# Picking each expert's tokens with the value columns stationary and the one-hot columns moving

## The chip, the cores and the metric

The kernel runs on one core of a Trainium2 chip. The metric is the device time of one execution in microseconds (us); lower is better. Engines are TensorE (PE, with its weight loads shown apart as PEld), VectorE (DVE), ScalarE (ACT), GpSimd (POOL) and SyncE (SP, which only issues DMAs here).

## The reference, cut to what matters

A graph layer over 1250 nodes and 21250 edges comes first; then a layer of 16 experts, in which every expert takes the 156 tokens with the largest affinity. The change touches only the choice of tokens in the second part:

```python
logits = jnp.einsum('bsd,de->bse', x, gate_weight)
affinity = jax.nn.softmax(logits, axis=-1).transpose(0, 2, 1)
gating, index = jax.lax.top_k(affinity, k)          # k = 156 of 1250 tokens
x_in = jnp.take_along_axis(x[:, None, :, :], index[..., None], axis=2)
h = jax.nn.gelu(jnp.einsum('bekd,edh->bekh', x_in, w1) + b1[None, :, None, :])
x_e = jnp.einsum('bekh,ehd->bekd', h, w2) + b2[None, :, None, :]
weighted = gating[..., None] * x_e
out = out.at[jnp.arange(Bx)[:, None], idx_flat].add(vals_flat)
```

## The kernel before, in words

The program has four stretches: layer norm and a table of rows in DRAM; 34 steps over the edges; two dense layers with batch norm; and, from about 397 us, the gate and the experts. Every engine has its own instruction list, written out by hand, and they meet through semaphores (`wait_ge`, `then_inc`). There is no scheduler: the order of the calls in `expert(e)` of each engine is the order of its work.

At the end of the gate, `slot` holds for each of the 1250 tokens (125 partitions by NT = 10 tiles) and each expert the place that the token takes among the expert's K = 156, or a number that matches no place. Then, for each expert e:

- `choose(e)` on VectorE (L1148 to L1155) makes the one-hot matrix `pick`: ten `tensor_scalar` compare `iota_slot` with the slot of a tile's tokens, 125 tokens by 156 places in fp16 each.
- `pick_tokens(e)` on TensorE (L1459 to L1467) multiplies it with `tok_aff`, which holds three values for a token and expert: the token's number and its affinity in two fp16 parts. The stationary operand is a half of `pick` (125 by KH = 78) and the moving one `tok_aff` (125 by 3). There are two halves and ten tiles, so 20 matmuls; the result `picked` lies in bank 1 as 78 partitions by 6.
- `indices(e)` on VectorE (L1157 to L1165) makes from it the gate values `gat` (through `gat_high`) and the row numbers `idx`: three short instructions.
- `gather(e)` on GpSimd (L466) fetches the 156 token rows by two indirect DMAs into `xg`, a ring of four; `turn_rows(e)` (L1469) turns them with eight transposes into banks 1 and 0, and `columns(e)` copies one bank by VectorE (L1167) and one by ScalarE (L704).
- `up(e, half)` (L1478) is 16 fp32 matmul instructions for each half, `gelu` on ScalarE and `low_h` on VectorE (L1181) make the hidden values in two fp16 parts, and `down(e)` (L1489, its matmuls are in `product`, L1300) is 48 fp16 matmuls of 156 moving columns. Its second half waits for `h_low` of the second half, which `low_h(e, 1)` gives.
- `turn_back(e)` (L1504) turns the result with eight transposes, `weigh` on VectorE and ScalarE multiplies by the gate, and `scatter` on GpSimd adds the rows into the output.

TensorE's order in `expert(e)` is `up(e, 0)`, `pick_tokens(e + 3)`, `turn_back(e - 1)`, `up(e, 1)`, `turn_rows(e + 1)`, `down(e)`. VectorE's is `indices(e + 3)`, `weigh(e - 1)`, `low_h(e, 0)`, `choose(e + 4)`, `columns(e + 1)`, `low_h(e, 1)`, `down_low(e + 1)`. So picks run three experts ahead. The picks of experts 0 to 2 stand in front of the loop, with `indices(0)` to `indices(2)` interleaved with `choose(2)` and `choose(3)` on VectorE; `down_low(0)` and `columns(0)` follow them there. `turn_rows(e)` waits for `idx_ready` of the picks issued before it, since it writes bank 1, in which `picked` lies; for expert 0 that is the third one.

The last lines of `turn_rows` and of `pick_tokens` before the matmuls say this:

```python
pe.wait_ge(xg_in[e % XR], e // XR * 32 + 32)
pe.wait_ge(idx_ready, min(e + 3, EX))
pe.wait_ge(pick_ready, e + 1)
```

Of the kernel before, what the change touches and what calls it, by code (L numbers as in the profile page):

```python
# [8 lines left out]
F32 = mybir.dt.float32  # L9
# [9 lines left out]
def gnn_ffn_kernel(nc, x, src, dst, edge_attr, W_e, b_e, W1, b1, g1, beta1, W2, b2, g2, beta2, eps,  # L19
# [5 lines left out]
    NT = N // P  # L25
# [9 lines left out]
    EX = gate_w.shape[1]  # L35
    K = N // EX * 2
    KH = K // 2
# [37 lines left out]
    with ExitStack() as ctx:  # L75
        def sb(name, shape, dt):
            return ctx.enter_context(nc.sbuf_tensor(name, shape, dt))

        def sem(name):
            return ctx.enter_context(nc.semaphore(name))  # L80

        bank = [ctx.enter_context(nc.psum_tensor(f"bank{i}", [128, 512], F32)) for i in range(8)]
# [66 lines left out]
        ident = sb("ident", [128, 128], F32)  # L149
# [36 lines left out]
        tok_aff = sb("tok_aff", [P, NT, EX, 3], F16)  # L186
# [19 lines left out]
        slot = sb("slot", [P, EX, NT], F32)  # L206
        idx = sb("idx", [KH, EX, 2], U32)
        gat = sb("gat", [KH, EX, 2], F32)
        gat_high = [sb(f"gat_high{b}", [KH, 2], F32) for b in range(2)]

        silu = [aggT[:, i, 0:CH[2][1]] for i in range(HK)]
# [21 lines left out]
        pick, xg, xT, hT, h32, yT, yw = [], [], [], [], [], [], []  # L233
# [53 lines left out]
        assert 3 * N + NT * 128 <= NT * H  # L287
        aff_lanes = rows_z2[0:P, 2 * N:2 * N + NT * 128].rearrange("p (t e l) -> p t e l", t=NT, e=EX)

        picked = bank[1][0:KH, 320:326]  # L290
        b1c, g1c, be1c = (colA[:, i * F1:(i + 1) * F1] for i in range(3))
        b2c, g2c, be2c = (colA[:, 3 * F1 + i * HK:3 * F1 + (i + 1) * HK] for i in range(3))

# [25 lines left out]
        kept = sem("kept"); kth_ps = sem("kth_ps"); count_ps = sem("count_ps")  # L319
        above_ready = sem("above_ready"); above_ps = sem("above_ps"); taken_ready = sem("taken_ready")  # L320
        taken_ps = sem("taken_ps");
        pick_ready = sem("pick_ready"); pick_ps = sem("pick_ps"); idx_ready = sem("idx_ready")
        xg_in = [sem(f"xg_in{b}") for b in range(XR)]
        ew_in = [[sem(f"ew_in{b}{m}") for m in range(2)] for b in range(RH)]
        W1_hi = sem("W1_hi"); W1_lo = sem("W1_lo"); W2_hi = sem("W2_hi"); W2_lo = sem("W2_lo")
# [432 lines left out]
        def _(dve):  # L758
# [389 lines left out]
            def choose(e):  # L1148
# [5 lines left out]
                                             None, ALU.is_equal)  # L1154
                last.then_inc(pick_ready, 1)  # L1155

            def indices(e):  # L1157

                dve.wait_ge(pick_ps, e + 1)
                v = picked.rearrange("p (a c) -> p a c", a=2)  # L1160
                dve.tensor_scalar(gat_high[e % 2][:], v[:, :, 1], 1.0 / A_SCALE, None, ALU.mult).then_inc(gat_step, 1)
                dve.wait_ge(gat_step, e + 1)
                dve.scalar_tensor_tensor(out=gat[:, e, :], in0=v[:, :, 2], scalar=1.0 / A_SCALE, in1=gat_high[e % 2][:],
                                         op0=ALU.mult, op1=ALU.add).then_inc(gat_ready, 1)
                dve.tensor_copy(idx[:, e, :], v[:, :, 0]).then_inc(idx_ready, 1)  # L1165
# [15 lines left out]
            def low_h(e, half):  # L1181
                b, f = e % 2, slice(half * 2, half * 2 + 2)
                dve.wait_ge(h_high, e * 2 + half + 1)
                dve.tensor_tensor(hT[b][:, 1, f, :], h32[b][:, f, :], hT[b][:, 0, f, :],
                                  ALU.subtract).then_inc(h_low, 1)
# [8 lines left out]

            def expert(e):
                if e + 3 < EX:
                    indices(e + 3)
                if e >= 1:
                    weigh(e - 1)
                low_h(e, 0)  # L1200
                if e + 4 < EX:
                    choose(e + 4)
                if e + 1 < EX:
                    columns(e + 1)
                low_h(e, 1)
                if e + 1 < EX:
                    down_low(e + 1)
# [2 lines left out]
            choose(0)  # L1210
            choose(1)
            for e in range(3):
                indices(e)
                if e < 2:
                    choose(e + 2)
# [8 lines left out]
        def _(pe):  # L1224
            pe.wait_ge(consts, 5)

            for n, (i, bk) in enumerate(((1, bank[5]), (0, bank[2]))):
                pe.wait_ge(ends_f_ready, n + 1)
                for j in range(J):
                    last = pe.transpose(bk[0:P, j * SB:(j + 1) * SB],  # L1230
                                        ends_f[i].rearrange("s (p j) -> s j p", j=J)[:, j, :], ident[0:SB, 0:SB])
# [12 lines left out]
            for t in range(2):  # L1244
# [4 lines left out]
                      start=True, stop=True).then_inc(zero_ps, 1)  # L1249
# [94 lines left out]
            for k in range(HK):  # L1344
                pe.wait_ge(h_hi, k + 1)
                for f in range(F1):
                    pe.matmul(bank[f][:, 0:nn], W1_16[:, 0, k, f * 128:(f + 1) * 128], h16[:, 0, k, :],  # L1347
                              start=(k == 0), stop=False, skip_group_check=True)
            pe.wait_ge(h_lo, 1)
            for f in range(F1):  # L1350
                for i, j in ((1, 0), (0, 1)):
                    for k in range(HK):
                        last = pe.matmul(bank[f][:, 0:nn], W1_16[:, i, k, f * 128:(f + 1) * 128], h16[:, j, k, :],  # L1353
                                         start=False, stop=(j == 1 and k == HK - 1), skip_group_check=True)
# [104 lines left out]
            def pick_tokens(e):  # L1459
                pe.wait_ge(pick_ready, e + 1)  # L1460
                if e >= 1:
                    pe.wait_ge(idx_ready, e)
                for a in range(2):
                    for t in range(NT):
                        last = pe.matmul(picked[:, 3 * a:3 * a + 3], pick[e % 2][:, t, a * KH:(a + 1) * KH],  # L1465
                                         tok_aff[:, t, e, :], start=(t == 0), stop=(t == NT - 1))
                last.then_inc(pick_ps, 1)  # L1467

            def turn_rows(e):  # L1469
                pe.wait_ge(xg_in[e % XR], e // XR * 32 + 32)  # L1470
                pe.wait_ge(idx_ready, min(e + 3, EX))
                for a in (1, 0):
                    for k in range(HK):
                        last = pe.transpose(bank[a][:, k * KH:(k + 1) * KH],  # L1474
                                            xg[e % XR][:, a, k * 128:(k + 1) * 128], ident[0:KH, 0:KH])
                    last.then_inc(xT_ps, 1)

            def up(e, half):  # L1478
                if half == 0:
                    pe.wait_ge(xT_sb, e * 2 + 2)  # L1480
                    pe.wait_ge(ew_in[e % RH][0], e // RH * 16 + 16)
                for f in range(half * 2, half * 2 + 2):
                    for k in range(HK):
                        last = pe.matmul(bank[2 + half][:, f % 2 * K:(f % 2 + 1) * K],  # L1484
                                         e32[e % RH][:, 0, k, f * 128:(f + 1) * 128], xT[e % 2][:, k, :],
                                         start=(k == 0), stop=(k == HK - 1), skip_group_check=True)
                    last.then_inc(h_ps, 1)
# [16 lines left out]
            def turn_back(e):  # L1504
                pe.wait_ge(yT_sb, e * HK + HK)
                for a in range(2):
                    if e >= 1:
                        pe.wait_ge(yw_ready[a], e)
                    for k in range(HK):
                        last = pe.transpose(bank[6 + a][0:KH, k * 128:(k + 1) * 128],  # L1510
                                            yT[e % 2][:, k, a * KH:(a + 1) * KH], ident[:])
                    last.then_inc(yt_ps, 1)

            def expert(e):
                up(e, 0)
                if e + 3 < EX:
                    pick_tokens(e + 3)
                if e >= 1:
                    turn_back(e - 1)
                up(e, 1)  # L1520
                if e + 1 < EX:
                    turn_rows(e + 1)
                down(e)

            for e in range(3):
                pick_tokens(e)
            turn_rows(0)
            for e in range(EX):
                expert(e)
# [27 lines left out]
```

## Time and profile before

| | |
|---|---|
| median of 3 runs | 645.5 us (642.93 to 646.48) |
| profiled execution, its own time | 645.98 us |
| profiled execution, span from first to last instruction | 644.2 us |
| TensorE busy | 518.5 us, 80% of the span |
| VectorE busy | 417.6 us, 65% |
| ScalarE busy | 344.0 us, 53% |
| GpSimd busy | 305.7 us, 47% |
| TensorE's mean granted clock | 0.917 of full speed |

The difference of 1.78 us between the profiled execution's time and its span lies around the instructions. The page has busy shares by stretch, the chain of work that ended last (each step followed back to what released it), and the groups of instructions with the idle time ahead of them. A piece of that chain lasts until the work is complete, while in the timeline instructions of one engine overlap; a matmul's own duration there (177 ns for a pick) is a latency, and what it costs in a row of them is the piece of the chain divided by their number. A granted clock of 0.50 is 1.2 GHz, 1.00 is 2.4 GHz.

### The profile page before, as it was taken

The numbers are of one execution on the slowest core, as the hardware profiler recorded it, in microseconds if no ns is written. First come the engines' busy times: TensorE is split into PE (matmuls) and PEld (weight loads), VectorE is DVE, ScalarE is ACT, GpSimd is POOL, SyncE is SP. The second block draws the span as 40 slices with busy tenths as digits, with TensorE's granted clock in tenths as the row PEclk, the third lists the DMA queues.
The fourth block names the chain that finished last, engine by engine and source line by source line (L and its number), as shares of the span: only waits on it lengthen the run. The fifth ranks groups of instructions, "written<-read, shape, count | busy, mean of one in ns | idle before, by whom it ended". The sixth has DMA issues, their size and how long they took to land.

```text
span 644.2 us, 12158 instructions
## 1 busy us (share of the span) xinstructions
PE 518.5 (80%) x4071; PEld 362.8 (56%) x4071; DVE 417.6 (65%) x1053; ACT 344.0 (53%) x716; POOL 305.7 (47%) x249
## 2 busy tenths in 40 slices
PE   3468778999889989998899976710489999999990
PEld 2324333455555545554346535610489999999990
DVE  7547776666676667676479737778746666766530
ACT  3535665666666666666386216420026666666660
POOL 3278888787887878770000000000244555555531
PEclk9979997999999999999899997855569999999996
DMA  9799966777767777762657505750038999994422
GB/s 237 218 235 206 206 181 180 181 194 191 187 178 191 198 190 189 191 177 76 231 178 211 164 0 156 233 193 0 10 85 270 283 271 304 273 271 66 61 34 28
DMA packets 76089, 111.60 MB, mean 173 GB/s; under 512 B 32201, under 2 KB 36865, under 8 KB 76027
## 3 DMA queue, kind: packets, MB, share of 16 engines
q0 software_dynamic: 43712, 53.95, 34.7%
q1 hardware_dynamic: 32211, 56.70, 29.5%
q8 instruction: 33, 0.54, 0.4%
q14 instruction: 29, 0.24, 0.2%
q10 hardware_dynamic: 104, 0.17, 0.1%
HBM read 97.81 MB, written 12.79 MB: 172 GB/s over the span
## 4 chain that ended last, share of the span: by engine, by line
PE 50%; issue 16%; DVE 14%; ACT 7%; DMA 6%; POOL 2%; DVEq 2%; ACTq 1%; POOLq 0%; SPq 0%
PE bank L1300 18%; PE bank L1484 11%; PE bank L1277 6%; DVE bank L964 4%; DMA big<-node_rows,edge_home 4%; ACT big L609 2%; PE bank L1291 2%; PE bank L1510 2%; PE bank L1293 2%; PE bank L1465 2%; PE bank L1474 1%; PE bank L1347 1%; PE bank L1353 1%; DVEq L924 1%; PE bank L1286 1%
## 5 line engine op out<-in xcount | busy, mean ns | idle before, releaser
L609 ACT ACTIVATE big<-bank 125x512 f32<-125x512 f32 x170 | 101.3, 596 | 98.0 <-DVE bank L964 51.2
L472 POOL DMA_INDIRECT big<-token_rows,idx x32 | 37.5, 1172 | 211.6 <-DVE idx L1165 206.1
L462 POOL DMA_INDIRECT big<-node_rows,edge_home x90 | 110.4, 1226 | 48.1 <-issue 47.8
L1277 PE MATMUL bank<-big,edge_home 125*64 125x256 f32 x688 | 100.0, 404 | 30.9 <-ACT big L609 24.5
L462 POOL DMA_INDIRECT pair<-node_rows,edge_home x80 | 100.7, 1259 | 24.4 <-issue 23.8
L1300 PE MATMUL bank<-big,pair 128*128 128x156 f16 (+2 forms) x1056 | 106.5, 260 | 1.1 <-DVE big L1016 0.9
L1300 PEld LDWEIGHTS bank<-big,pair 128*128 128x128 f16 x1056 | 81.0, 97 | 24.5 <-issue 1.4
L964 DVE SCALAR_TENSOR_TENSOR bank<-big,bank 125x512 f32<-125x512 f32 x90 | 60.0, 704 | 38.3 <-PE bank L1293 22.8
L1277 PEld LDWEIGHTS bank<-big,edge_home 125*64 125x64 f32 x688 | 41.0, 138 | 77.0 <-ACT big L609 43.1
L964 DVE SCALAR_TENSOR_TENSOR bank<-pair,bank 125x512 f32<-125x512 f32 x80 | 54.7, 722 | 32.6 <-PE bank L1293 17.3
L481 POOL DMA_INDIRECT out<-rows_z,idx x32 | 51.7, 1617 | 44.1 <-issue 24.9
L1291 PE MATMUL bank<-edge_home 128*125 128x512 f16 x170 | 69.0, 406 | 4.2 <-issue 4.2
L1293 PE MATMUL bank<-edge_home 66*125 66x512 f16 x170 | 66.9, 394 | 0.0
L712 ACT ACTIVATE big<-bank,colB 128x156 f32<-128x156 f32 x64 | 21.5, 387 | 47.6 <-PE bank L1484 42.3
L1291 PEld LDWEIGHTS bank<-edge_home 128*125 128x125 f16 x170 | 23.9, 140 | 28.5 <-issue 23.2
L1300 PE MATMUL bank<-rows_z 128*128 128x250 f16 x288 | 35.4, 271 | 0.0
L1300 PEld LDWEIGHTS bank<-rows_z 128*128 128x128 f16 x288 | 26.2, 98 | 11.8 <-issue 9.2
L1484 PE MATMUL bank<-big,raw 128*128 128x156 f32 x192 | 31.7, 325 | 0.5 <-ACT big L706 0.5
L1484 PEld LDWEIGHTS bank<-big,raw 128*128 128x128 f32 x192 | 29.7, 213 | 0.8 <-ACT big L706 0.8
L706 ACT ACTIVATE big<-bank 128x312 f32<-128x312 f32 x16 | 6.7, 416 | 43.4 <-PE bank L1474 43.3
L1153 DVE TENSOR_SCALAR big<-iota_slot,slot 125x156 f16<-125x156 f16 x160 | 29.1, 268 | 0.0
L1293 PEld LDWEIGHTS bank<-edge_home 66*125 66x125 f16 x170 | 24.1, 142 | 6.0 <-issue 0.8
(232 smaller groups left out, 904.9 us busy)
## 6 DMA issues: line engine op xcount, KB each, us to landing
raw<-in_L_ffn_w SPq DMA_DIRECT2D x12, 1024.0 KB
edge_home<-in_L_ffn_w SPq DMA_DIRECT2D x6, 1024.0 KB
pair<-in_L_ffn_w SPq DMA_DIRECT2D x6, 1024.0 KB
pair<-in_edge_attr SPq DMA_DIRECT2D x36, 140.0 KB
xs_home<-in_x SPq DMA_DIRECT2D x10, 448.0 KB
xs_home<-in_L_ffn_w SPq DMA_DIRECT2D x4, 1024.0 KB, 7.9
aggT<-in_L_ffn_w SPq DMA_DIRECT2D x4, 1024.0 KB, 9.4
node_rows<-rows_z SPq DMA_DIRECT2D x5, 448.0 KB
```

The source lines that it names most:

```text
L462: pool.indirect_dma_start(row(i % RING, j), None, node_rows, bass.IndirectOffsetOnAxis(src_i[:, i, j:j + 1], 0)).then_inc(row_in[i % RING] ...
L472: pool.indirect_dma_start(xg[e % XR][:, a, :], None, token_rows, bass.IndirectOffsetOnAxis(idx[:, e, a:a + 1], 0)).then_inc(xg_in[e % XR], 16)
L481: pool.indirect_dma_start(out, bass.IndirectOffsetOnAxis(idx[:, e, a:a + 1], 0), yw[e % YR][:, a, :], None, compute_op=ALU.add).then_inc(y ...
L609: act.activation(msg[:, b * J + j, :], bank[j][0:P, :], ACT.Relu).then_inc(msg_ready, 1)
L712: act.activation(h32[e % 2][:, f, :], bank[2 + half][:, f % 2 * K:(f % 2 + 1) * K], ACT.Gelu_apprx_tanh, bias=colB[:, e * HK + f:e * HK + ...
L964: dve.scalar_tensor_tensor(out=bank[j][0:P, :], in0=row(i % RING, j), scalar=E_SCALE, in1=bank[j][0:P, :], op0=ALU.mult, op1=ALU.add).then ...
L1153: last = dve.tensor_scalar(pick[e % 2][:, t, :], iota_slot[:], slot[:, e, t:t + 1], None, ALU.is_equal)
L1277: last = pe.matmul(bank[6 + b][a * WIN:(a + 1) * WIN, 0:H // 2], onehot[b][:, j, :], msg[:, b * J + j, a * (H // 2):(a + 1) * (H // 2)], s ...
L1291: pe.matmul(bank[j][0:P, :], edge_T[b][:, j, 0:P], We_hi[:], start=True, stop=False, skip_group_check=True)
L1293: pe.matmul(bank[j][0:P, :], edge_hi_T[b][:, j, 0:P], We_lo[0:ED + 2, :], start=False, stop=True, skip_group_check=True).then_inc(edge_ps, 1)
L1300: last = pe.matmul(bk, weights(i, k), values(j, k), start=(begin and p == k == 0), stop=(end and p == 2 and k == n - 1), skip_group_check= ...
L1484: last = pe.matmul(bank[2 + half][:, f % 2 * K:(f % 2 + 1) * K], e32[e % RH][:, 0, k, f * 128:(f + 1) * 128], xT[e % 2][:, k, :], start=(k ...
```

## The change

The operands of the pick change places. `tok_aff` (3 columns) is stationary and a tile of `pick` (156 columns) moves, so ten matmuls give the result lying down: 3 partitions by 156, in `picked_T` (bank 1, columns 320 to 475). A new VectorE step, `picked_copy(e)`, copies it to SBUF as fp32 (`picked_sb`, two buffers), and a new TensorE step, `turn_picked(e)`, turns its two halves with two fp32 transposes into `picked`, which now lies in columns 480 to 485 of the bank. `indices(e)` waits for the turned values.

```diff
--- before.py
+++ after.py
@@ -206,6 +206,7 @@
         slot = sb("slot", [P, EX, NT], F32)
         idx = sb("idx", [KH, EX, 2], U32)
         gat = sb("gat", [KH, EX, 2], F32)
+        picked_sb = [sb(f"picked_sb{b}", [3, K], F32) for b in range(2)]
         gat_high = [sb(f"gat_high{b}", [KH, 2], F32) for b in range(2)]
 
         silu = [aggT[:, i, 0:CH[2][1]] for i in range(HK)]
@@ -287,7 +288,8 @@
         assert 3 * N + NT * 128 <= NT * H
         aff_lanes = rows_z2[0:P, 2 * N:2 * N + NT * 128].rearrange("p (t e l) -> p t e l", t=NT, e=EX)
 
-        picked = bank[1][0:KH, 320:326]
+        picked_T = bank[1][0:3, 320:320 + K]
+        picked = bank[1][0:KH, 480:486]
         b1c, g1c, be1c = (colA[:, i * F1:(i + 1) * F1] for i in range(3))
         b2c, g2c, be2c = (colA[:, 3 * F1 + i * HK:3 * F1 + (i + 1) * HK] for i in range(3))
 
@@ -319,7 +321,7 @@
         kept = sem("kept"); kth_ps = sem("kth_ps"); count_ps = sem("count_ps")
         above_ready = sem("above_ready"); above_ps = sem("above_ps"); taken_ready = sem("taken_ready")
         taken_ps = sem("taken_ps");
-        pick_ready = sem("pick_ready"); pick_ps = sem("pick_ps"); idx_ready = sem("idx_ready")
+        pick_ready = sem("pick_ready"); pick_ps = sem("pick_ps"); pick_sb = sem("pick_sb"); pick_turned = sem("pick_turned"); idx_ready = sem("idx_ready")
         xg_in = [sem(f"xg_in{b}") for b in range(XR)]
         ew_in = [[sem(f"ew_in{b}{m}") for m in range(2)] for b in range(RH)]
         W1_hi = sem("W1_hi"); W1_lo = sem("W1_lo"); W2_hi = sem("W2_hi"); W2_lo = sem("W2_lo")
@@ -1154,9 +1156,13 @@
                                              None, ALU.is_equal)
                 last.then_inc(pick_ready, 1)
 
+            def picked_copy(e):
+                dve.wait_ge(pick_ps, e + 1)
+                dve.tensor_copy(picked_sb[e % 2][:], picked_T).then_inc(pick_sb, 1)
+
             def indices(e):
 
-                dve.wait_ge(pick_ps, e + 1)
+                dve.wait_ge(pick_turned, e + 1)
                 v = picked.rearrange("p (a c) -> p a c", a=2)
                 dve.tensor_scalar(gat_high[e % 2][:], v[:, :, 1], 1.0 / A_SCALE, None, ALU.mult).then_inc(gat_step, 1)
                 dve.wait_ge(gat_step, e + 1)
@@ -1194,10 +1200,12 @@
 
             def expert(e):
                 if e + 3 < EX:
-                    indices(e + 3)
+                    picked_copy(e + 3)
                 if e >= 1:
                     weigh(e - 1)
                 low_h(e, 0)
+                if e + 3 < EX:
+                    indices(e + 3)
                 if e + 4 < EX:
                     choose(e + 4)
                 if e + 1 < EX:
@@ -1210,6 +1218,7 @@
             choose(0)
             choose(1)
             for e in range(3):
+                picked_copy(e)
                 indices(e)
                 if e < 2:
                     choose(e + 2)
@@ -1460,11 +1469,17 @@
                 pe.wait_ge(pick_ready, e + 1)
                 if e >= 1:
                     pe.wait_ge(idx_ready, e)
+                for t in range(NT):
+                    last = pe.matmul(picked_T, tok_aff[:, t, e, :], pick[e % 2][:, t, :],
+                                     start=(t == 0), stop=(t == NT - 1))
+                last.then_inc(pick_ps, 1)
+
+            def turn_picked(e):
+                pe.wait_ge(pick_sb, e + 1)
                 for a in range(2):
-                    for t in range(NT):
-                        last = pe.matmul(picked[:, 3 * a:3 * a + 3], pick[e % 2][:, t, a * KH:(a + 1) * KH],
-                                         tok_aff[:, t, e, :], start=(t == 0), stop=(t == NT - 1))
-                last.then_inc(pick_ps, 1)
+                    last = pe.transpose(picked[:, 3 * a:3 * a + 3], picked_sb[e % 2][:, a * KH:(a + 1) * KH],
+                                        ident[0:3, 0:3])
+                last.then_inc(pick_turned, 1)
 
             def turn_rows(e):
                 pe.wait_ge(xg_in[e % XR], e // XR * 32 + 32)
@@ -1517,6 +1532,8 @@
                     pick_tokens(e + 3)
                 if e >= 1:
                     turn_back(e - 1)
+                if e + 3 < EX:
+                    turn_picked(e + 3)
                 up(e, 1)
                 if e + 1 < EX:
                     turn_rows(e + 1)
@@ -1524,6 +1541,7 @@
 
             for e in range(3):
                 pick_tokens(e)
+                turn_picked(e)
             turn_rows(0)
             for e in range(EX):
                 expert(e)
```

TensorE's instructions from `up(1, 0)` to `turn_rows(2)`, which stand for every later expert with a pick. Before (L1484 is `up`, L1465 the pick, L1510 `turn_back`, L1474 `turn_rows`, L1300 `down`):

```order
L1484 MATMUL bank<-big,raw 128x156 [waits ew_in10,xT_sb]
L1484 MATMUL bank<-big,raw 128x156 x7
L1465 MATMUL bank<-tok_aff,big 78x3 [waits idx_ready,pick_ready]
L1465 MATMUL bank<-tok_aff,big 78x3 x19
L1510 MATMUL bank<-ident,rows_z 78x128 [waits yT_sb]
L1510 MATMUL bank<-ident,rows_z 78x128 x7
L1484 MATMUL bank<-big,raw 128x156 x8
L1474 MATMUL bank<-ident,big 128x78 [waits idx_ready,xg_in2]
L1474 MATMUL bank<-ident,big 128x78 x7
L1300 MATMUL bank<-big,pair_1 128x156 [waits h_low,yT_sb,down_lo]
L1300 MATMUL bank<-big,pair_1 128x156 x23
```

With the change (the lines have moved: L1499 `up`, L1473 the pick, L1525 `turn_back`, L1480 `turn_picked`, L1489 `turn_rows`):

```order
L1499 MATMUL bank<-big,raw 128x156 [waits ew_in10,xT_sb]
L1499 MATMUL bank<-big,raw 128x156 x7
L1473 MATMUL bank<-big,tok_aff 3x156 [waits idx_ready,pick_ready]
L1473 MATMUL bank<-big,tok_aff 3x156 x9
L1525 MATMUL bank<-ident,rows_z 78x128 [waits yT_sb]
L1525 MATMUL bank<-ident,rows_z 78x128 x7
L1480 MATMUL bank<-ident,picked_sb 78x3 [waits pick_sb]
L1480 MATMUL bank<-ident,picked_sb 78x3
L1499 MATMUL bank<-big,raw 128x156 x8
L1489 MATMUL bank<-ident,big 128x78 [waits idx_ready,xg_in2]
L1489 MATMUL bank<-ident,big 128x78 x7
```

Twenty picks have become ten, and two transposes that wait for VectorE (`pick_sb`) stand between `turn_back` and the second half of `up`.

VectorE's instructions for the same expert, before (L1161 to L1165 `indices`, L1178 `weigh`, L1184 `low_h`, L1153 `choose`, L1170 `columns`, L1191 `down_low`):

```order
L1161 TENSOR_SCALAR gat_high<-bank 78x2 [waits pick_ps]
L1163 SCALAR_TENSOR_TENSOR gat<-bank,gat_high 78x2 [waits gat_step]
L1165 CAST idx<-bank 78x2
L1178 TENSOR_SCALAR rows_z<-bank,gat 78x512 [waits yt_ps,gat_ready]
L1184 TENSOR_TENSOR big<-big 128x312 [waits h_high]
L1153 TENSOR_SCALAR big<-iota_slot,slot 125x156 [waits pick_ps]
L1153 TENSOR_SCALAR big<-iota_slot,slot 125x156 x9
L1170 COPY big<-bank 128x4x78 [waits xT_ps]
L1184 TENSOR_TENSOR big<-big 128x312 [waits h_high]
L1191 SCALAR_TENSOR_TENSOR pair_1<-edge_home,pair_1 128x512 [waits down_hi] x4
```

With the change (L1161 is now the copy, L1167 to L1171 `indices`, L1184 `weigh`, L1190 `low_h`, L1155 `choose`, L1176 `columns`, L1197 `down_low`):

```order
L1161 COPY picked_sb<-bank 3x156 [waits pick_ps]
L1184 TENSOR_SCALAR rows_z<-bank,gat 78x512 [waits yt_ps,gat_ready]
L1190 TENSOR_TENSOR big<-big 128x312 [waits h_high]
L1167 TENSOR_SCALAR gat_high<-bank 78x2 [waits pick_turned]
L1169 SCALAR_TENSOR_TENSOR gat<-bank,gat_high 78x2 [waits gat_step]
L1171 CAST idx<-bank 78x2
L1155 TENSOR_SCALAR big<-iota_slot,slot 125x156 [waits pick_ps]
L1155 TENSOR_SCALAR big<-iota_slot,slot 125x156 x9
L1176 COPY big<-bank 128x4x78 [waits xT_ps]
L1190 TENSOR_TENSOR big<-big 128x312 [waits h_high]
L1197 SCALAR_TENSOR_TENSOR pair_1<-edge_home,pair_1 128x512 [waits down_hi] x4
```

The copy stands where `indices` stood, and `indices` has moved behind the first `low_h`, ahead of `choose`.

VectorE in front of the loop, for the first two picks, before:

```order
L1161 TENSOR_SCALAR gat_high<-bank 78x2 [waits pick_ps]
L1163 SCALAR_TENSOR_TENSOR gat<-bank,gat_high 78x2 [waits gat_step]
L1165 CAST idx<-bank 78x2
L1153 TENSOR_SCALAR big<-iota_slot,slot 125x156 [waits pick_ps]
L1153 TENSOR_SCALAR big<-iota_slot,slot 125x156 x9
L1161 TENSOR_SCALAR gat_high<-bank 78x2 [waits pick_ps]
L1163 SCALAR_TENSOR_TENSOR gat<-bank,gat_high 78x2 [waits gat_step]
```

With the change:

```order
L1161 COPY picked_sb<-bank 3x156 [waits pick_ps]
L1167 TENSOR_SCALAR gat_high<-bank 78x2 [waits pick_turned]
L1169 SCALAR_TENSOR_TENSOR gat<-bank,gat_high 78x2 [waits gat_step]
L1171 CAST idx<-bank 78x2
L1155 TENSOR_SCALAR big<-iota_slot,slot 125x156 [waits pick_ps]
L1155 TENSOR_SCALAR big<-iota_slot,slot 125x156 x9
L1161 COPY picked_sb<-bank 3x156 [waits pick_ps]
```

Here the copy stands directly ahead of `indices`, which waits for TensorE's turn of it (`pick_turned`) with nothing in between.

## Rows read from the trace of the kernel before

**Rows 1.** Busy time by stretch (start:end, length, then each engine): an expert with a pick, one without
```profile
539.13:548.87 9.74, 9.74 (x119) 9.72 (x118) 6.65 (x22) 6.48 (x17) 5.42 (x5) 1.00 0.97 281
...
600.87:609.86 8.99, 8.99 (x97) 8.97 (x97) 4.61 (x9) 6.48 (x18) 4.01 (x3) 1.00 0.42 54
```
**Rows 2.** Chain of work that ended last: start us, us, what; one expert, and one without a pick
```profile
554.32 0.72 PE bank L1465 x20
555.04 0.91 PE bank L1510 x8
555.94 2.12 PE bank L1484 x16
558.07 0.54 PE bank L1474 x8
558.61 3.28 PE bank L1300 x48
...
603.03 0.87 PE bank L1510 x8
```
**Rows 3.** Timeline of VectorE, one expert of the loop: start us, us, instruction, idle before
```profile
545.33 0.15 DVE L1161 TENSOR_SCALAR gat_high<-bank 78x2 f32<-78x2 f32 x1 [2.17 <-PE bank L1465]
...
545.60 0.14 DVE L1165 CAST idx<-bank 78x2 uint32<-78x2 f32 x1
545.91 0.75 DVE L1178 TENSOR_SCALAR rows_z<-bank,gat 78x512 f32<-78x512 f32 x1 [0.16 <-PE bank L1510]
546.57 0.47 DVE L1184 TENSOR_TENSOR big<-big 128x312 f16<-128x312 f32 x1
546.97 1.84 DVE L1153 TENSOR_SCALAR big<-iota_slot,slot 125x156 f16<-125x156 f16 x10
548.73 0.47 DVE L1170 COPY big<-bank 128x312 f32<-128x312 f32 x1
549.56 0.48 DVE L1184 TENSOR_TENSOR big<-big 128x312 f16<-128x312 f32 x1 [0.36 <-ACT big L716]
```
**Rows 4.** Chain of work that ended last, before the loop and in expert 0
```profile
458.38 3.50 DVE big L1153 x20
...
462.14 0.08 DVE idx L1165
...
468.51 1.32 PE bank L1474 x8
...
469.85 0.44 ACT big L706
...
470.34 4.53 PE bank L1484 x16
474.86 1.27 PE bank L1465 x20
```
**Rows 5.** Timeline of VectorE before the loop: `columns(0)`
```profile
469.33 0.48 DVE L1170 COPY big<-bank 128x312 f32<-128x312 f32 x1 [0.61 <-PE bank L1474]
```
**Rows 6.** The same chain: a hand-over to a single matmul (L1437), and ten fp32 transposes (L1419)
```profile
440.61 0.05 issue
440.66 0.20 PE bank L1437
440.86 0.03 issue
...
416.33 1.22 PE bank L1419 x10
```
**Rows 7.** Busy time by stretch: columns as in rows 1; the clock is third from the end
```profile
403.73:407.95 4.22, 4.22 (x27) 3.16 (x28) 4.15 (x13) 0.95 (x3) 0.00 (x0) 0.50 0.53 175
407.95:410.30 2.35, 2.24 (x24) 1.56 (x21) 2.35 (x6) 1.09 (x3) 0.00 (x0) 1.00 0.47 132
476.13:479.69 3.56, 3.56 (x15) 3.56 (x15) 2.49 (x14) 0.00 (x0) 1.95 (x2) 0.51 0.00 0
479.69:483.96 4.27, 4.27 (x61) 4.27 (x60) 2.72 (x5) 3.76 (x10) 0.66 (x1) 1.00 0.75 211
```

## The prediction

> **What bounds the kernel now.** I read the busy shares by stretch first. While the experts run, TensorE is busy for all of the 9.74 us that one expert takes, at the full clock, and VectorE for 6.65 us [rows 1]. So the chain of waits is read next, and it is TensorE alone: pick 0.72, `turn_back` 0.91, half of `up` 2.12, `turn_rows` 0.54, `down` 3.28 us, piece after piece with no gap [rows 2]. What the change adds to or takes from TensorE's list comes out one for one, in each expert that picks inside the loop (13: experts 0 to 12 pick 3 to 15). VectorE waits 2.17 us for the pick and 0.36 us later in the turn [rows 3]; it has room, but not everywhere. Before the loop the picture is another: there the chain goes through VectorE, the gather and the first transposes [rows 4], and TensorE waits.
>
> **The loop, part by part.** Twenty picks go: 0.72 us [rows 2], 36 ns each. Ten come with 156 moving fp16 columns, which is what a matmul of `down` has: 3.28 / 48 = 68 ns [rows 2], so 0.68 us. The three-column weights should load behind the matmul before. That is -0.04 us; the lowest price I can give is 156 columns at 2.4 GHz, 0.65 us.
>
> `turn_back` behind a pick takes 0.91 us and without one 0.87 [rows 2]; behind a long matmul its first weights are loaded in time, -0.04 us.
>
> Two transposes are new. Their stationary operand has 78 columns, their moving one 3, as in the old pick, but in fp32. The floor is the old pick's 36 ns. The ceiling comes from ten fp32 transposes with 125 stationary and 32 moving columns, 1.22 us, 0.122 each [rows 6]; by columns 78/125 of it, 76 ns. I take 50 ns, nearer to the row with the same sizes: +0.10 us, bounds 0.07 to 0.15. Behind them the first weights of `up`, 128 fp32 columns, are no longer covered by a long matmul; by the 0.04 us of `turn_back`, whose weights are 78 columns, I take +0.05 us, bounds 0 to 0.12.
>
> The sum is -0.04 - 0.04 + 0.10 + 0.05 = +0.07 us for an expert, bounds -0.07 to +0.19. Times the 12 experts at full clock: **+0.8 us, bounds -0.8 to +2.3**. The change halves the count of picks and saves nothing, because the old ones were so short that they paid for 78 stationary columns, and the new ones pay for 156 moving ones.
>
> The Trainium skill (TensorE: Matmul & The Clock Gate, "LDWEIGHTS (loading the stationary operand)") puts a load at the columns divided by 1.2 GHz. By that the old picks would be at least 20 times 65 ns, an estimate of 1.30 us, and the exchange would save some 0.5 us an expert; the trace disagrees with it at 36 ns, and the sum goes by the trace. The rival that would follow has its own place below.
>
> **The waits in the loop.** TensorE's transposes wait for the copy. VectorE stands idle when the pick ends and starts at once [rows 3]. A copy of 312 elements out of PSUM takes 0.47 us and an operation on 2 takes 0.15 [rows 3]; 156 elements lie halfway, 0.31 us. `turn_back` covers it with 0.91 us, and the copy ends before VectorE's `weigh` starts (0.58 us after the start of `indices` before). So both are hidden; were `turn_back` not there, it would be a gap, which is the case of expert 0.
>
> `indices` takes 545.33 to 545.74, 0.42 us, and moves behind the first `low_h`. Queued behind it are `choose`, `columns` and the second `low_h`, on which the second half of `down` waits. That `low_h` starts at 549.56 because ScalarE is late, with VectorE idle for 0.36 us ahead of it, and ends at 550.04 [rows 3]; the second half of `down` starts half of its 3.28 us after about 548.8, near 550.4. Slack 0.36 + 0.36 = 0.7 us against 0.42: hidden, with 0.3 us left. `turn_rows` waits for `idx`, which comes at about 547.5, against its start near 548.3: hidden with 0.8 us. The gather starts 1.7 us later than before, but three experts ahead of its use, 29 us; GpSimd is busy for 5.42 of 9.74 us [rows 1], and the scatter behind the gather has one and more experts to its deadline. Nothing on SP's queue moves, and the last three experts and the tail are as they were.
>
> **Before the loop.** Here nothing covers the round trip. The first two `choose` end at 461.88 and `idx` is there at 462.22 [rows 4]. Now each of the three turns has on VectorE: the copy 0.31, the hand-over 0.05, a lone short matmul 0.20 and back 0.03 [rows 3, 6], with about 0.1 more for the second transpose (the old picks were 1.27 / 20 = 64 ns apart at half clock). That is 0.69 us a turn, bounds 0.5 to 0.9, and 2.07 us for three. `down_low(0)` and `columns(0)` are queued behind. `columns(0)` had 0.61 us of idle time ahead of it, and ended at 469.81 where ScalarE's copy ended at 470.29 [rows 4, 5], so 1.09 us is free: `up(0, 0)` starts 2.07 - 1.09 = 0.98 us later, at 471.3 (bounds 0.5 to 1.6). The gather, on the other path to it, is only 0.69 later. In expert 0 no `turn_back` stands between pick and turn. TensorE then waits out its own drain (about 0.15), 0.03, the copy 0.31 and 0.05, and turns at half clock, about 0.2; the picks give back 0.1. That is 0.6 to 0.7 us.
>
> Together 1.65 us at half clock. All this lies ahead of 479.7, where the granted clock went from 0.50 to 1.00 [rows 7]. If the rise stays at its time, work that is pushed over it runs twice as fast, and the delay costs half: **+0.85 us**; if the rise moves with the work, all of it, 1.65.
>
> **Sum.** 645.98 + 0.8 + 0.85 = 647.6 us against the profiled execution; the median of the runs shown is 0.5 us below that execution, so **647.2 us** is forecast, +1.7. A measurement of this kernel tells about 0.5% (3.2 us) from no change.
>
> **The rivals.** *The clock rises earlier.* Before, TensorE worked without a gap from 470.34 and got the full clock only at 479.69, 9.35 us later; an earlier stretch got it after 4.22 us of work without a gap, 403.73 to 407.95 [rows 7]. In the 9.35 us lie 1.27 us of picks with 3 moving columns [rows 4]; now they move 156. If 4.2 us of `up` and new picks are enough, the rise comes at 471.3 + 4.2 = 475.5: half of 4.2 us is gained, 0.5 us is half of the late start, the gap of expert 0 costs some 0.6, and the loop 0.8, which gives 645.5 - 2.1 + 0.5 + 0.6 + 0.8 = 645.3. For it speaks that nothing else in the stretch is thin; against it that the later start brings a new gap. The Trainium skill (TensorE: Matmul & The Clock Gate, Part 1) says that the point of the rise differs from run to run of one kernel; the three runs spread over 3.55 us, which agrees but does not show it. Chance 0.22.
>
> *VectorE's moved step holds back `down` (slower).* The place is `low_h(e, 1)`. It decides from where the moved step adds more than the 0.7 us of slack instead of 0.42: if `pick_turned` came 0.3 us after the first `low_h` ends, because the turns sit behind all of `turn_back`. By the rows the turns end near 546.4 and that `low_h` at 547.04 [rows 3], so there is 0.6 us of room; each tenth past it costs 11 experts 0.1. At 0.3 us late beyond the slack it is 3.3 us more: 650.5. Chance 0.12.
>
> *The exchange saves what the thin picks cost at half clock (faster).* There the twenty took 1.27 us [rows 4]. Were that their true price in the loop, with half a microsecond hidden in their neighbours' pieces, each expert would gain 1.27 - 0.68 - 0.15 + 0.04 = 0.48, twelve 5.8: 645.5 - 5.8 + 0.85 = 640.6. Against it: an expert without a pick takes 8.99 us and one with it 9.74 [rows 1], 0.75 apart, so no hidden half exists. The rule on loads cited above from the Trainium skill (TensorE: Matmul & The Clock Gate) would give a saving of this kind. Chance 0.03.
>
> **How the numbers follow.** The forecast has the remaining 0.63. Its own bounds are the loop's -0.8 to +2.3 and for the start half of 0.5 + 0.6 to the whole of 1.6 + 0.7: 645.2 to 650.1. With the early clock and the spread of the median itself (the three runs lie 2.6 below and 1 above theirs) the range is 643.8 to 649.8. Slower by over 0.5% is the second rival and the top end of the forecast, 0.12 + 0.02; faster is the third and a lucky case of the first, 0.05; the same is 0.81.
>
> **What would show it.** Ten picks of 0.68 us and two transposes of 0.1 between `turn_back` and `up`; an expert of 9.8 us in the loop; a copy of 0.31 us; the first `up` at 471.3; a gap of about half a microsecond in expert 0. An expert of 9.5 us or less, or a wait of `down` for `low_h`, makes it wrong. A rise near 475.5 is the first rival.

## The result and the profile after

The changed kernel takes 651.32 us (median of 6 runs, 650.36 to 654.17), the kernel before 645.64 (6 runs, 642.93 to 646.48). The ratio is 1.0101, with a 95% interval of 1.0073 to 1.0128: slower by 1.0%, 5.7 us, outside the range that was given. The profiled execution took 650.54 us with a span of 648.7, against 645.98 and 644.2.

The chain of waits of one expert in the loop, start us, us, what (L1499 `up`, L1473 the pick, L1525 `turn_back`, L1480 the turn, L1489 `turn_rows`, L1309 `down`):

```profile
554.27 2.16 PE bank L1499 x16
556.43 0.78 PE bank L1473 x10
557.21 1.00 PE bank L1525 x8
558.21 0.17 PE bank L1480 x2
558.38 2.32 PE bank L1499 x16
560.70 0.54 PE bank L1489 x8
561.24 3.28 PE bank L1309 x48
```

Against [rows 2] the pick went from 0.72 to 0.78, `turn_back` from 0.91 to 1.00, the second half of `up` from 2.12 to 2.32, and the turn is new with 0.17: +0.52 us. The first half of `up`, `turn_rows` and `down` stayed. TensorE still waits for nobody; it has 10.25 us of work where it had 9.74 [rows 1]:

```profile
550.99:561.24 10.25, 10.25 (x111) 9.74 (x110) 6.83 (x23) 6.46 (x17) 5.33 (x5) 1.00 0.98 269
```

The third number of this row is the time in which weight loads are at work: 9.74 of the 10.25 us, where it was 9.72 of 9.74. The timeline of the weight loads (PEld) of the same expert (start us, us, instruction, idle time before) says where they stand still:

```profile
556.36 0.64 PEld L1473 LDWEIGHTS bank<-big,tok_aff 125*3 125x3 f16 x10 [0.17 <-issue]
557.14 0.81 PEld L1525 LDWEIGHTS bank<-ident,rows_z 128*78 128x78 f32 x8
558.14 0.15 PEld L1480 LDWEIGHTS bank<-ident,picked_sb 3*78 3x78 f32 x2 [0.19 <-issue]
558.31 0.43 PEld L1499 LDWEIGHTS bank<-big,edge_home 128*128 128x128 f32 x3
```

and the matmuls:

```profile
556.36 0.85 PE L1473 MATMUL bank<-big,tok_aff 125*3 125x156 f16 x10
557.14 1.07 PE L1525 MATMUL bank<-ident,rows_z 128*78 128x128 f32 x8
558.14 0.24 PE L1480 MATMUL bank<-ident,picked_sb 3*78 3x3 f32 x2
558.31 0.53 PE L1499 MATMUL bank<-big,edge_home 128*128 128x156 f32 x2
```

In each of the four pairs the first load starts together with the first matmul. In the kernel before the same rows read otherwise. The loads and the matmuls of the old pick:

```profile
554.02 0.93 PEld L1465 LDWEIGHTS bank<-tok_aff,big 125*78 125x78 f16 x20
...
554.15 0.88 PE L1465 MATMUL bank<-tok_aff,big 125*78 125x3 f16 x20
```

There the load runs 0.13 us ahead of its matmul, under the work in front of it; the first load of `turn_back` starts 0.04 us ahead (554.86 and 554.90) and that of `up` 0.11 (555.67 and 555.78). Within the ten new picks loads do run ahead. Only where the operands change from full-size ones to those of 3 columns (the pick) or 3 partitions (the turn), or back, does the next load begin late.

The kernel before has such a change too, in the steps over the edges, which this change does not touch. L1277 there has 64 stationary columns, L1293 has 125 columns and is 66 partitions deep:

```profile
53.20 0.14 PEld L1293 LDWEIGHTS bank<-edge_home 66*125 66x125 f16 x1
53.72 0.20 PEld L1277 LDWEIGHTS bank<-big,edge_home 125*64 125x64 f32 x4 [0.39 <-issue]
...
53.41 0.38 PE L1293 MATMUL bank<-edge_home 66*125 66x512 f16 x1
53.73 0.65 PE L1277 MATMUL bank<-big,edge_home 125*64 125x256 f32 x4
```

Behind another full-size matmul the load of L1293 runs 0.21 us ahead of its own. The load of L1277 does not run ahead, and neither does the one behind it (the load and the matmul of L1291 both start at 47.00). A stationary operand of 36 partitions (L1264) does the same to the full-size one behind it (L1265), which waits for no semaphore: its load and its matmul both start at 32.31.

Before the loop and in expert 0 (`choose` to the first half of `up`, the pick, the turn, the second half):

```profile
457.57 3.50 DVE big L1155 x20
...
470.48 4.46 PE bank L1499 x16
474.95 0.79 PE bank L1473 x10
...
475.76 0.32 DVE picked_sb L1161
...
476.12 0.24 PE bank L1480 x2
...
479.22 3.29 PE bank L1309 x48
```

In the busy shares by stretch the granted clock is the third number from the end:

```profile
470.48:474.75 4.27, 4.27 (x16) 4.14 (x16) 0.00 (x0) 0.00 (x0) 2.29 (x3) 0.50 0.37 102
474.75:479.22 4.47, 4.07 (x41) 3.72 (x40) 3.04 (x16) 1.63 (x5) 1.27 (x1) 1.00 0.04 14
```

The two profiled executions compare like this, the changed kernel first:

- Up to the first `choose`: 457.57 against 458.38 us, -0.8. Nothing there was changed.
- From it to the first `up`: 12.91 against 11.96, +0.95.
- From there to the start of `down(0)`: 8.74 against 10.34, -1.6, because the clock rose 4.3 us after the first `up` began and not 9.3.
- From there to the start of expert 14: 135.30 against 129.18, +6.1, which is 12 experts of 0.51.

Together that is +4.7, and the spans differ by 4.5.

### The profile page after: what moved, and what is told of

It reads as the page before. It is cut to its first block, busy times and chain, and to the rows that moved or that the text cites. A ratio compares the mean times of both kernels' runs of the same rounds, so it can differ in the third digit from the quotient of the medians.

```text
span 648.7 us, 11918 instructions
## 1 busy us (share of the span) xinstructions
PE 525.2 (81%) x3943; PEld 361.4 (56%) x3943; DVE 420.3 (65%) x1069; ACT 344.3 (53%) x716; POOL 306.3 (47%) x249
## 4 chain that ended last, share of the span: by engine, by line
PE 53%; DVE 16%; issue 15%; ACT 7%; DMA 3%; DVEq 2%; POOL 2%; ACTq 1%; POOLq 0%; SPq 0%
PE bank L1309 18%; PE bank L1499 11%; PE bank L1286 7%; DVE bank L966 3%; PE bank L1525 2%; PE bank L1300 2%; PE bank L1302 2%; ACT big L611 2%; DMA big<-node_rows,edge_home 2%; PE bank L1473 2%; DVEq L926 1%; PE bank L1356 1%; PE bank L1362 1%; PE bank L1489 1%; PE bank L1295 1%
## 5 line engine op out<-in xcount | busy, mean ns | idle before, releaser
L1309 PE MATMUL bank<-big,pair 128*128 128x156 f16 (+2 forms) x1056 | 106.5, 260 | 1.1 <-DVE big L1018 0.9
L1309 PEld LDWEIGHTS bank<-big,pair 128*128 128x128 f16 x1056 | 80.9, 97 | 24.5 <-issue 1.4
L1300 PE MATMUL bank<-edge_home 128*125 128x512 f16 x170 | 68.9, 406 | 3.8 <-issue 3.8
L1300 PEld LDWEIGHTS bank<-edge_home 128*125 128x125 f16 x170 | 23.8, 140 | 28.2 <-issue 22.8
L1309 PE MATMUL bank<-rows_z 128*128 128x250 f16 x288 | 35.4, 271 | 0.0
L1309 PEld LDWEIGHTS bank<-rows_z 128*128 128x128 f16 x288 | 26.2, 98 | 11.9 <-issue 9.2
L1499 PE MATMUL bank<-big,raw 128*128 128x156 f32 x192 | 30.3, 315 | 1.0 <-DVE big L1176 1.0
L1155 DVE TENSOR_SCALAR big<-iota_slot,slot 125x156 f16<-125x156 f16 x160 | 28.9, 255 | 0.0
L1499 PEld LDWEIGHTS bank<-big,raw 128*128 128x128 f32 x192 | 27.8, 202 | 1.3 <-DVE big L1176 1.2
```

What stands on the lines that cost most here:

```text
L1155: last = dve.tensor_scalar(pick[e % 2][:, t, :], iota_slot[:], slot[:, e, t:t + 1], None, ALU.is_equal)
L1300: pe.matmul(bank[j][0:P, :], edge_T[b][:, j, 0:P], We_hi[:], start=True, stop=False, skip_group_check=True)
L1309: last = pe.matmul(bk, weights(i, k), values(j, k), start=(begin and p == k == 0), stop=(end and p == 2 and k == n - 1), skip_group_check= ...
```

## The experiments

The theory after the result (the expectations call it the shape theory): TensorE does not load weights ahead across a change between a small and a full-size stationary operand. The rivals are that the cost belongs to the swapped operands, to fp32, to the transpose mode, or to the number of columns that are loaded. Every ratio below is to the kernel before as it was timed again beside that run.

**The pick 96 columns wide.** The stationary operand takes 93 more columns of the same table (it was given 128 spare columns of zeros at its end):

```diff
-last = pe.matmul(picked_T, tok_aff[:, t, e, :], pick[e % 2][:, t, :],
+last = pe.matmul(bank[1][0:96, 320:320 + K], tok_aff_home[:, (t * EX + e) * 3:(t * EX + e) * 3 + 96], pick[e % 2][:, t, :],
```

> The changed kernel, its pick with a stationary operand of 96 columns in place of 3 (the three value columns and 93 columns behind them, whose products nobody reads). Shape theory: TensorE does not load weights ahead across a change between a small and a full-size stationary operand, and each such change costs about 0.1 us; in an expert of the changed kernel there are four (into the pick +0.09, out of it +0.13, into the turn +0.09, out of it +0.14). Then the two at the pick go: pick 0.78 to 0.69 us, turn_back 1.00 to 0.87, an expert 10.25 to 10.03 us, the whole 2.6 us faster than the changed kernel. Rival (operands or the wait in front of the pick are the cause, whatever the width): 0.78, 1.00 and 10.25 us stay.

Measured: 645.65 us against 643.14, ratio 1.0039 (1.0006 to 1.0073). The chain, and the timeline of the weight loads:

```profile
563.64 0.69 PE bank L1476 x10
564.32 0.88 PE bank L1528 x8
```

```profile
563.34 0.81 PEld L1476 LDWEIGHTS bank<-big,tok_aff_home 125*96 125x96 f16 x10
```

The first load of the pick starts at 563.34, with no idle time ahead of it, and its first matmul at 563.47. The pick and `turn_back` fell as expected to 0.69 and 0.88, an expert takes 10.04 us, and the turn, which was left alone, costs what it did (0.17 us, with 2.32 for the half of `up` behind it). Loading 32 times the columns made the step shorter. Whole-kernel times, with intervals of 0.3% (2 us) to either side, cannot tell the 2.6 us that were expected from the 4 us by which the ratios differ; the pieces of the chain decide here and below.

**The turn in fp16.** Two plain matmuls with an fp16 identity replace the fp32 transposes, at a depth of 3 partitions:

```diff
-last = pe.transpose(picked[:, 3 * a:3 * a + 3], picked_sb[e % 2][:, a * KH:(a + 1) * KH], ident[0:3, 0:3])
+last = pe.matmul(picked[:, 3 * a:3 * a + 3], picked_sb[e % 2][:, a * KH:(a + 1) * KH], ident16[0:3, 0:3], start=True, stop=True)
```

> The changed kernel, its turn in fp16 by two plain matmuls with a fp16 identity (the values are exact in fp16), 3 partitions deep as before. Shape theory: the turn costs what it did, 0.17 us, and the half of up behind it 2.32 us: the expert stays at 10.2 us. Rival (the cost around the turn is that of fp32 or of the transpose mode): the half of up goes back to 2.12 to 2.15 us and the expert to 10.0 us.

Measured: 649.5 us, ratio 1.0099 (1.0066 to 1.0131); the changed kernel had 1.0101.

```profile
565.07 0.16 PE bank L1481 x2
565.23 2.32 PE bank L1500 x16
```

Neither fp32 nor the transpose mode is the cause.

**The same turn 96 partitions deep**, with zeros under the three rows (`TURN_R = 96` for `picked_sb` and `ident16[0:TURN_R, 0:3]`, cleared once at the start):

> As the run with the fp16 turn of 3 partitions, but the turn's operands are 96 partitions deep (93 rows of zeros under the three). Shape theory: the two changes of shape at the turn go, turn about 0.10 us, the half of up behind it 2.15, an expert about 10.0 us. Rival (depth does not matter, only width of the stationary operand does): as the run with 3 partitions, 10.2 us.

Measured: 644.73 us, ratio 1.0028 (0.9998 to 1.0058).

```profile
564.10 0.04 PE bank L1483 x2
564.14 2.23 PE bank L1502 x16
```

The turn went from 0.16 to 0.04 us and the half of `up` from 2.32 to 2.23, a little above the 2.15 expected; an expert takes 10.03 us. The depth of a small operand matters as its width does.

**Both.**

> Both: the pick 96 columns wide and the fp16 turn 96 partitions deep. Shape theory: all four changes of shape are gone, an expert takes 9.8 us and the kernel is within 0.3% of the one before (my blind sum for the loop was +0.07 us an expert). If the two are not additive, something else holds TensorE: an expert of 9.9 us or more.

Measured: 642.49 us, ratio 0.9997 (0.9964 to 1.0029).

```profile
559.57 0.69 PE bank L1479 x10
560.26 0.88 PE bank L1531 x8
561.13 0.04 PE bank L1486 x2
561.18 2.23 PE bank L1505 x16
```

An expert takes 9.82 us. The two savings add up to 0.43 of the 0.51 us; the 0.08 that is left is near the +0.07 of the prediction's sum. The values that are used are those of the changed kernel.

**The cost of one small operand by itself.** The kernel before got one extra matmul between `turn_back` and the second half of `up`, with three shapes of its stationary operand: 128 partitions by 78 columns (shown), `ones16[0:128, 0:3]`, and `ones16[0:3, 0:78]`.

```diff
+pe.matmul(bank[0][0:78, 500:503], ones16[0:128, 0:78], ones16[0:128, 0:3], start=True, stop=True)
```

> The kernel before with one extra fp16 matmul in each expert, between turn_back and the second half of up: 128 partitions deep, 78 stationary and 3 moving columns of ones, into a corner of bank 0 that nobody reads. It is the control for the next two. All theories: about 0.04 us for the matmul and up to 0.11 for the weights of up that it leaves uncovered (the half of up was 2.23 in place of 2.12 behind the full-size turn): an expert of 9.85 to 9.9 us.

> The same extra matmul with 3 stationary columns in place of 78. Shape theory: one small operand between full-size ones costs two changes of shape, about 0.2 us over the control, although its weights are 26 times narrower: an expert of 10.0 to 10.1 us. Rival (a cost by columns loaded): an expert no longer than the control's.

> The same extra matmul, 3 partitions deep with 78 stationary columns. Shape theory: as with 3 columns, about 0.2 us over the control, 10.0 to 10.1 us an expert. Rival (only width counts): as the control.

Measured in single executions of 668.18, 664.58 and 672.11 us, on a chip on which the kernel before had a median of 661.7 (14 runs, 653 to 667). These times say nothing about steps of 0.2 us; the pieces of the chain do, and those that were left alone have their usual lengths there (first half of `up` 2.16, pick 0.72, `turn_back` 0.91). 78 columns:

```profile
577.25 0.00 PE bank L1520
577.26 2.23 PE bank L1484 x16
```

3 columns:

```profile
572.15 0.10 PE bank L1520
572.25 2.32 PE bank L1484 x16
```

3 partitions:

```profile
569.59 0.12 PE bank L1520
569.71 2.32 PE bank L1484 x16
```

The full-size matmul adds 0.11 us to an expert, all of it in the half of `up` behind it (2.23 against 2.12), whose first load now starts 0.03 us ahead of its matmul in place of 0.11. Either small one adds 0.19 to 0.21 more, about half of it in its own piece and half in the one behind. So the narrow load costs more than the wide one, on both sides of it.

**Where the border lies.**

> The changed kernel with 64 stationary columns in the pick in place of 3. If a small operand is one that fills at most half of the array's columns, it costs what 3 columns cost: pick 0.78, turn_back 1.00 us. If only the smallest sizes are special, it costs what 96 columns cost: 0.69 and 0.88 us.

> The same with 65 columns, one more than half of the array. If the border lies at half: pick 0.69 and turn_back 0.88 us, as with 96. If the cost fades with width: between those and 0.78 and 1.00 us.

64 columns (a single execution, 647.11 us), pick and `turn_back`:

```profile
563.10 0.80 PE bank L1476 x10
563.90 1.00 PE bank L1528 x8
```

65 columns (646.06 us):

```profile
562.99 0.69 PE bank L1476 x10
563.67 0.88 PE bank L1528 x8
```

One column makes 0.23 us, in single executions, but with the same pieces in the neighbouring experts to 0.01 us. For the width the border lies between 64 and 65 columns, half of the 128. For the depth the experiments have 3 and 96 partitions; with the rows of the kernel before shown above, 36 stop the load-ahead and 66 do not, and where between them the border lies was not tried.

One thing stays open: whether TensorE only holds the next load back at such a change or first finishes what is under way. No run here separates the two.

**The old pick with full operands.** The kernel before, its one-hot operand read 128 columns wide; the columns past the half of 78 are the neighbour's and give rows that nobody reads:

```diff
-last = pe.matmul(picked[:, 3 * a:3 * a + 3], pick[e % 2][:, t, a * KH:(a + 1) * KH],
+last = pe.matmul(bank[1][0:128, 320 + 3 * a:323 + 3 * a], pick_home[e % 2][:, t * K + a * KH:t * K + a * KH + 128],
```

> The kernel before, still 20 picks with the one-hot stationary and 3 columns moving, but each stationary operand is 128 columns of the one-hot (50 more than the half that is used) in place of 78. In the traces a load of 128 fp16 columns lasts 97 ns and one of 78 lasts 116 to 119, so full operands may load faster. If the load sets the spacing of the picks, they come 37 ns apart or less: at 25 to 30 ns the pick takes 0.5 to 0.6 us in place of 0.72 and the kernel gains 2 to 3 us. Rival (a load costs by its columns): 128/78 of 36 ns, 59 ns apart, the pick takes 1.2 us and the kernel is 6 us slower than before.

Measured: 657.26 us against 661.7 on that chip, ratio 0.9949 (0.9912 to 0.9987). The pick in the chain, and the durations of its loads (min/median/max ns), first in the kernel before (L1465) and then in this run (L1469):

```profile
568.01 0.48 PE bank L1469 x20
```

```profile
L1465 PEld LDWEIGHTS bank<-tok_aff,big x320: 116/119/189, 460.2 to 593.8; 125*78 125x78 f16 x160
...
L1469 PEld LDWEIGHTS bank<-tok_aff,big x320: 95/96/152, 477.5 to 607.3; 125*128 125x128 f16 x160
```

The 20 picks take 0.48 us, 24 ns apart in place of 36, and an expert takes 9.51 us in place of 9.74. The Trainium skill (TensorE: Matmul & The Clock Gate, "Weight-path perf modes — Fast Weight Load (FWL) and DoubleRow") says that a faster load is used when the operand has 128 weights and is not fp32. The trace agrees: a load of 128 columns lasts 96 ns where one of 78 lasted 119.

**The clock.** In both kernels the first `up` runs at half clock, and the pick of expert 3 follows it. In this run only that pick was moved:

```diff
 up(e, 0)
-if e + 3 < EX:
+if 1 <= e < EX - 3:
     pick_tokens(e + 3)
...
 up(e, 1)
+if e == 0:
+    pick_tokens(3)
```

> The kernel before, in which only the pick of expert 3 is moved, from between the two halves of up in expert 0 to behind them. Clock theory: the 20 picks with 3 moving columns there put off the rise of the granted clock (9.3 us after the first up began, in the kernel before; 4.2 to 5.5 us in the five kernels whose picks move 156 columns). Then the rise comes at most 6.8 us after the first up begins and the kernel is 0 to 2 us faster, the rest of the loop being the same. Rival (the spread of the rise is chance and the picks have no part in it): a rise near 9 us can be seen here too.

Measured: 644.01 us against 643.01, ratio 1.0025 (0.9994 to 1.0056): no gain. The rise came 5.7 us after the first `up` began, as expected, but much of what it gave went into new waits. The chain, and TensorE's timeline behind the late pick:

```profile
468.11 7.28 PE bank L1484 x32
475.39 0.73 PE bank L1465 x20
...
479.06 0.40 DVE big L1184
```

```profile
476.70 0.74 PE L1474 MATMUL bank<-ident,big 78*128 78x78 f32 x8 [0.60 <-DVE idx L1165]
...
479.51 1.81 PE L1300 MATMUL bank<-big,pair 128*128 128x156 f16 x24 [0.43 <-DVE big L1184]
```

`turn_rows(1)` waited 0.60 us for `idx` of the late pick. `indices(3)` also stands at the head of VectorE's list for expert 0, so `low_h`, `choose`, `columns` and the second `low_h` came after the late pick, and the second half of `down` waited 0.43 us for them. The expectation had counted neither wait.

The cause of the early rise stays open. In the nine profiles in which no picks with 3 moving columns stood between the halves of `up` it came 3.9 to 6.1 us after the first `up` began; in the five that had them there it came after 9.3, 8.9, 5.0, 9.3 and 6.2 us. That fits the clock theory and, with two of five early, does not show it.

**The last two together.**

> The kernel before with the 128 columns wide one-hot as stationary operand (pick 0.48 us in place of 0.72, and 0.5% faster than before when it was timed) and the pick of expert 3 behind both halves of up. It should beat both kernels: 3 us from the picks in the loop and 0 to 2 us from the clock, a ratio of 0.992 to 0.996 to the kernel before.

Measured: 638.21 us against 643.01, ratio 0.9943 (0.9915 to 0.997), which is the wide pick's own gain; the moved pick added nothing that can be told. Both kernels with the wide pick beat the kernel before by about 0.5%.

## Why the prediction was wrong, point by point

- **What bounds the kernel: right.** The loop is TensorE's, and what was added to its list came out one for one, +0.51 us in each of 12 experts.
- **The ten picks at 68 ns: right, and not the whole.** The starts of the new picks lie 68 ns apart. The step failed in its next sentence, "the three-column weights should load behind the matmul before": the first one did not, and the piece was 0.78 in place of 0.68. The sum took the weight load of a small operand as free; the run with 96 columns, 0.69 us, shows that having few columns was what cost.
- **`turn_back` -0.04: wrong sign.** It was +0.09, since its first load, too, starts late behind a small operand. With 65 and with 96 columns it is 0.87 to 0.88, the value that I had forecast.
- **The turn +0.10 and the weights of `up` +0.05: too small.** They were 0.17 and 0.20, both beyond their bounds. Without the change of shape, and with the turn in fp16, they are 0.04 and 0.11. Their sum of 0.15 is what was forecast, but by luck: the turn lies below its bounds of 0.07 to 0.15, and the weights of `up` cost twice what was taken.
- **The step that failed: a change of shape was put at nothing.** In the run without small operands an expert takes 9.82 us, the 9.8 of the prediction. The missing term is the stopped load-ahead at four places, 0.43 us an expert by the runs, 5.2 us in the loop, where the whole sum had +0.8 and an upper bound of +2.3. The bounds left it out because the nearest rows that I took, 78 by 3 in fp16 and 32 by 125 in fp32, were read within a row of like instructions, where the cost of a change does not show. The trace of the kernel before had it all the same, at each passage between L1277 and its full-size neighbours.
- **The waits in the loop: right.** The copy took 0.31 us under `turn_back` and TensorE waited for neither it nor `low_h`. The slower rival (VectorE holds back `down`, 650.5 us) has nearly the measured time by luck: its wait did not occur.
- **Before the loop: right.** The first `up` began 0.95 us later after the first `choose` (forecast 0.98), and the gap in expert 0 is there, 0.40 us of waiting and 0.24 for the turn (forecast 0.6 to 0.7 together).
- **The clock: what the rival named came about in the profiled execution.** The rise came 4.3 us after the first `up` began (the rival had 4.2), and the stretch to `down(0)` became 1.6 us shorter, gap and turn included. The prediction gave it a chance of 0.22. That the moving columns of the pick brought it about is not shown.
- **The sum.** For the profiled execution 647.6 us was forecast and 650.54 measured, 2.9 more: the loop took 5.3 us more than forecast, the start 1.5 us less because of the early clock, and the part ahead of the first `choose`, where nothing was changed, 0.8 us less. Without these two the miss would have been larger. The prediction's own bounds reached 650.1 and its range ended at 649.8; the median of 651.32 lies above both.
- **The faster rival: refuted.** The old picks had no hidden cost, and in the run without small operands, too, an expert takes 9.82 us against 9.74.

## What to carry to other kernels

When a step whose stationary operand has few rows or columns is put between full-size matmuls, count the change of shape on both sides (here about 0.1 us each) and not only the step. Look for it in a trace at the first load behind such a change: does it start ahead of its matmul or with it? A mean over a row of like instructions hides it.

Padding the stationary operand took that cost away here: to 65 or more columns, with products that nobody reads, or to 96 partitions, with zeros. Padding an fp16 operand from 78 to all 128 columns made its load faster as well.

Before swapping operands, compare the two steps by the spacing of their matmuls in a trace. Here 20 at 36 ns became 10 at 68 ns, which saves nothing.

## What the runs showed of the hardware that was not expected

- 64 stationary columns cost 0.23 us more for pick and `turn_back` than 65 (0.80 and 1.00 against 0.69 and 0.88).
- A stationary operand 3 partitions deep stops the load-ahead as one of 3 columns does: +0.21 and +0.19 us for a single matmul over the same one at full size. In the kernel before, one of 36 partitions stops it and one of 66 does not.
- 20 matmuls with 128 fp16 stationary columns and 3 moving ones run 24 ns apart; with 78 stationary columns they run 36 ns apart.
